# Cross attention, row maximum: from one subtraction on VectorE to the bias of eight exponentials on ScalarE

## The reference

```
ln_out = _ln(hidden_states, ln_w, ln_b)
qx = _ln(_fp8_linear_pertensor(ln_out, wqx, ...).reshape(b, s, g, hpg, d), qxln_w, qxln_b)
kx, vx = jnp.split(jnp.einsum('bsi,oi->bso', cond, w_kv_x), 2, axis=-1)
kx = _ln(kx.reshape(b, sc, g, d), kxln_w, kxln_b)
scores = jnp.einsum('bsghd,btgd->bghst', q, k) * scale      # scale = d ** -0.5, d = 128
p = jax.nn.softmax(scores, axis=-1)                         # over 64 keys
xout = jnp.einsum('bghst,btgd->bsghd', p, v)
catq = _div_clamp_fp8(cat, proj_smooth)                     # then the output projection
```

## Time and profile before

| | us |
|---|---|
| median of 3 runs | 748.12 |
| the profiled execution | 748.93 |
| its span (first to last instruction) | 747.2 |
| PE busy | 613.6 (82%) |
| DVE busy | 505.7 (68%) |
| ACT busy | 378.6 (51%) |
| POOL busy | 359.5 (48%) |
| mean granted PE clock, full = 1 | 0.914 |

### The profile page before, as it was taken

One profiled execution on the slowest core, in us unless ns is written; L12 is line 12 of the kernel. 1 busy time (PEld: TensorE's weight loads), 2 busy tenths in 40 slices (PEclk: granted clock), 3 DMA queues, 4 the chain that ended last, 5 costly groups with the idle time before them and its releaser, 6 DMA issues. The chain is left out here.

```text
span 747.2 us, 10815 instructions
## 1 busy us (share of the span) xinstructions
PE 613.6 (82%) x3735; PEld 492.0 (66%) x3738; DVE 505.7 (68%) x945; ACT 378.6 (51%) x663; POOL 359.5 (48%) x288
## 2 busy tenths in 40 slices
PE   4677996587787999999988788888863599999994
PEld 2544334443566788887877777778763578888883
DVE  5689767694587888888888798888852253333432
ACT  1545666862683655556567366666510333333420
POOL 3321444000656656657468765555631644445541
PEclk9897998698798999999999799999985599999998
DMA  7940211023320010201551111111001211111001
GB/s 258 308 145 14 100 76 49 16 100 128 113 85 1 29 57 1 85 2 52 174 170 25 49 49 51 57 58 57 2 0 53 75 43 43 43 43 42 0 1 57
DMA packets 36212, 50.66 MB, mean 68 GB/s; under 512 B 8257, under 2 KB 22465, under 8 KB 36161
## 3 DMA queue, kind: packets, MB, share of 16 engines
q1 hardware_dynamic: 36160, 50.00, 20.2%
HBM read 37.41 MB, written 12.58 MB: 67 GB/s over the span
## 5 line engine op out<-in xcount | busy, mean ns | idle before, releaser
L1236 POOL TENSOR_TENSOR g_rs<-g_ve,neg_half 128x4 f32<-128x4 f32 x96 | 100.5, 1053 | 98.3 <-DVE g_ve L1309 82.8
L1638 PE MATMUL g_proj<-w_hi,g_xqc 128*128 128x512 f32 x192 | 86.9, 453 | 8.0 <-POOL g_xqc L1231 5.5
L1247 POOL TENSOR_TENSOR g_cat<-g_big,g_kb 128x1024 fp32r<-128x1024 bf16 x32 | 68.4, 2138 | 43.9 <-DVE g_big L1359 43.2
L1309 DVE TENSOR_REDUCE g_ve<-g_sq 128x4 f32<-128x516 f32 x96 | 64.4, 681 | 31.2 <-ACT g_sq L1471 31.2
L1661 PE MATMUL g_turn<-ident,g_qn 128*128 128x128 f32 x384 | 59.6, 282 | 24.9 <-DVE g_qn L1315 12.8
L1638 PE MATMUL g_proj<-w_lo,g_xqc 128*128 128x512 f32 x192 | 79.8, 415 | 0.0
L1672 PE MATMUL g_scores<-g_qkT 128*128 128x64 f32 x512 | 66.6, 287 | 13.0 <-DVE g_ex L1325 13.0
L1672 PEld LDWEIGHTS g_scores<-g_qkT 128*128 128x128 f32 x512 | 64.9, 205 | 18.4 <-issue 18.0
L1900 POOL TENSOR_TENSOR m_h_lo<-m_h,m_h_hi 128x512 fp32r<-128x512 f32 x32 | 40.7, 1289 | 70.7 <-ACT m_h_hi L1947 70.7
L1471 ACT ACTIVATE g_sq<-g_proj 128x512 f32<-128x512 f32 x80 | 47.8, 598 | 49.0 <-PE g_proj L1638 46.0
L1661 PEld LDWEIGHTS g_turn<-ident,g_qn 128*128 128x128 f32 x384 | 44.8, 144 | 37.1 <-DVE g_qn L1315 16.0
(11 more groups left out here) (214 smaller groups left out, 1648.9 us busy)
## 6 DMA issues: line engine op xcount, KB each, us to landing
kvx_rows<-f_kept SPq DMA_DIRECT2D x32, 256.0 KB, 2.4
g_kraw<-kvx_rows SPq DMA_DIRECT2D x16, 256.0 KB, 3.2
g_v<-kvx_rows SPq DMA_DIRECT2D x8, 512.0 KB, 4.6
m_raw<-in_L_W SPq DMA_DIRECT2D x16, 256.0 KB, 3.5
c_raw<-in_L_wqT SPq DMA_DIRECT2D x4, 512.0 KB, 8.8
f_w_ctx<-in_L_wkvxT SPq DMA_DIRECT2D x4, 512.0 KB, 7.7
x_raw<-in_L_wqxT SPq DMA_DIRECT2D x4, 512.0 KB, 3.7
c_praw<-in_L_wprojT SPq DMA_DIRECT2D x4, 512.0 KB, 6.4
```

The lines of the kernel that those rows point to most:

```text
L1236: G.tensor_tensor(rs[:, i % 2, :], ve[:, i % 2, :], k["half"][:, 0:4], ALU.pow).then_inc(q["rs_done"], 1)
L1247: G.tensor_tensor(cat[:, h].rearrange("p h (b s) -> p b h s", b=2), big[:, h, :].rearrange("p (b h s) -> p b h s", b=2, s=SEQ), kb[:, h, : ...
L1309: V.tensor_reduce(ve[:, i % 2, :], sq[:, i % 2], AX.X, ALU.add).then_inc(q["ve_done"], 1)
L1638: last = T.matmul(bank(n, i)[:], xqc[:, n % 2, view * KT + c_, :], w[:, c_, :], start=c_ == 0 and part == 0, stop=c_ == KT - 1 and part == 1)
```

## The change

For cross tiles alone, `less_max` keeps its reduction, but in place of the subtraction it multiplies the 8 maxima by -d^-0.5 in place, which makes them a bias. `exponent` then runs eight exponentials, one for each block of 64 columns, each of which reads the scores from PSUM with its own column of `g_mx` as bias. The last of the eight raises `exp_done`. The bank of scores is now free when ACT has read it, so for cross tiles `scores` waits for `exp_done` where it waited for `sub_done`. The wait for `pt_done` (that the earlier content of `g_ex` has been transposed) goes from DVE to ACT.

```diff
                     V.tensor_reduce(mx[:, h, :], s3, AX.X, ALU.max).then_inc(q["max_done"], 1)
                     dve.wait_ge(q["max_done"], n * 2 + h + 1)
+                    if cross(n):
+                        V.tensor_scalar(mx[:, h, :], mx[:, h, :], -(D ** -0.5), None, ALU.mult).then_inc(q["sub_done"], 1)
+                        return
                     if n > 0:
                         dve.wait_ge(q["pt_done"], n * 2 + h - 1)
...
                 def exponent(n, h):
                     act.wait_ge(q["sub_done"], n * 2 + h + 1)
+                    if cross(n):
+                        act.wait_ge(q["pt_done"], n * 2 + h - 1)
+                        for g in range(2 * GH):
+                            at = slice(g * SEQ, (g + 1) * SEQ)
+                            last = A.activation(ex[:, h, at], sp_[:, at], ACT.Exp, bias=mx[:, h, g:g + 1], scale=D ** -0.5)
+                        last.then_inc(q["exp_done"], 1)
+                        return
                     A.activation(ex[:, h, :], ex[:, h, :], ACT.Exp, scale=D ** -0.5).then_inc(q["exp_done"], 1)
...
                 def scores(n, h):
                     pe.wait_ge(q["tev_done"], n * NN + (h + 1) * NN // 2)
-                    if n > 0 or h > 0:
+                    if cross(n if h > 0 else n - 1):
+                        pe.wait_ge(q["exp_done"], n * 2 + h)
+                    elif n > 0 or h > 0:
                         pe.wait_ge(q["sub_done"], n * 2 + h)
```

## The result

| | before | after |
|---|---|---|
| median of 4 runs each | 747.75 us (746.99 to 748.54) | 784.08 us (782.76 to 787.28) |
| profiled execution | 748.93 | 785.01 |
| its span | 747.2 | 783.3 |
| mean granted PE clock | 0.914 | 0.896 |

The changed kernel is slower by a factor of 1.049 (95% interval 1.046 to 1.053). The forecast was 784 us.

The account below looks back on a forecast made before the run. A cross-tile loop over DVE and PE was taken to bound the kernel, neither engine alone. Wait 20.7, tile 8 2.3, clock 12.5 and 0.6 make 36.1 us on 748.12: 784 us, own range 777 to 791, with rivals 765 to 793.

Parts of the forecast that it names:

- The loop: Cross tile: half 0's reduction and subtraction, PE from second scores to transpose, then DVE; delaying those scores lengthens it one for one.
- the rival on the faster side: Cross tiles: DVE's own work sets the tile and 8.3 us of it are gone, 739.8 us; chance 0.015.
- Step 1: Half 0's multiplication on DVE in cross tiles is held until POOL's running g_cat ends: 1.6 us instead of 0.17.
- near 0.2 for half 1: Sign in the profile after: half 1's multiplication takes near 0.2 us, against about 1.6 us for half 0.
- Step 2: ACT's eight exponentials of 64 columns, starting 0.244 us apart, take 2.04 us where one took 0.63.
- The rival without overlap: ACT's eight exponentials do not overlap: 5.3 us more, 789 us; chance 0.06.
- Step 3: Reduction's start to PE's second scores grows from 1.56 to 4.52 us: 2.96 us per tile, 20.7 over tiles 9 to 15.
- Step 4: Tile 8: DVE's wait ends with POOL, whose root ends later, so the scaling starts 2.3 us later.
- Step 5: PE's clock falls after a 3.4 us gap: 2.5 us in each of tiles 10 to 14, 12.5; tiles 9 and 15, 0.6.
- The sum: Whole kernel: 20.7 + 2.3 + 12.5 + 0.6 = 36.1 us more, added to the median of 748.12.
- the signs: Profile after, cross tiles: tile of 25 to 26 us, clock 0.50 in each tile's scores, DVE's second-scaling wait about 6 us.

Follow-up runs that it names:

- Experiment 4: Kernel before, with PE's scores in cross tiles waiting for the exponential of the half before instead of the subtraction: 753.9 us, ratio 1.009.
- experiment 5: Kernel before, with the change made in half 1 of cross tiles alone; half 0 keeps subtraction, one exponential and early release: 747.6 us, ratio 1.000.
- experiment 1: Changed kernel, with the multiplication of the 8 maxima on ACT instead of DVE: 762.1 us, ratio 1.020 to the kernel before.
- experiment 2: Kernel before, with the multiplication of the maxima added on DVE in cross tiles, its result unread: 766.2 us, ratio 1.027.
- experiment 3: Kernel before, with the 512-column exponential in cross tiles cut into eight of 64 on SBUF without bias, subtraction kept: 747.75 us, ratio 1.000.
- experiment 11: Changed kernel, with 24 unread matmuls filling PE's gap before the second scores in tile 8 too, besides tiles 9 to 14: 768.6 us, ratio 1.028.
- Experiment 6: Changed kernel, with 24 unread matmuls filling PE's gap before the second scores of tiles 9 to 14: 772.3 us, ratio 1.032 to the kernel before.
- 7: Changed kernel, with one exponential of 512 columns in place of the eight, first block's maximum as bias for all: 773.7 us, ratio 1.034.

## Why the prediction was right, step by step

- **The loop.** Right. Experiment 4 moved the release by 0.66 us and the tile by 0.67; experiment 5 left both alone and the time with them. The 0.5 us less work of DVE in each half 1 brought nothing there, and in the changed kernel DVE stands still for 6.8 us of a tile; the rival on the faster side falls with that.
- **Step 1, the hold.** Right in size: 1.60 us on record, to 0.02 us after POOL's end. Shown from both sides: taken away (experiment 1) and added to the kernel before (2). The exclusive lock of the Trainium skill (SBUF — State Buffer, Who interferes with whom) agrees with these rows. The sign "near 0.2 for half 1" held in seven of the eight tiles and not in tile 8 (1.02 us), where the hold was overlooked. What runs here do not show is which condition of the instruction puts it under the lock.
- **Step 2, the exponentials.** The mechanism was right, but the term of 2.04 us was too large: it measured 1.74. One takes 0.33 us as the sum had it, but they start (1.74 - 0.33) / 7 = 0.20 us apart, not 0.244. Without a bias column, from SBUF, they took 1.28 (experiment 3). The estimate from the budget of the Trainium skill (ScalarE: Activation LUTs, Rules for kernel authors), 2.8 us, was further off. The rival without overlap is out.
- **Step 3, the wait.** 4.24 - 1.56 = 2.68 us per tile for 2.96 predicted, by step 2's 0.3. In tiles 9 to 15 that is 18.8 for 20.7. One sign was wrong: DVE's wait before its second scaling was to be about 6 us and is 3.87, since another 2.30 us are spent ahead of the second reduction.
- **Step 4, tile 8.** 4.2 us for 2.3. POOL's delay alone is 27.05 - 25.33 = 1.7 (experiment 11); the other 2.5 are the clock, which I had at 0 there, with 2.3 as its upper end.
- **Step 5, the clock.** Right. It fell in all five of tiles 10 to 14, and the stream grew by 1.55 + 3.11 + 2.70 + 3.10 + 2.65 = 13.1 us for 12.5. One sign was only partly met: the clock was not at 0.50 over the scores of each tile. They took 3.64 us in tiles 12 and 14, but 2.40 to 2.89 in 10, 11 and 13, and tile 10 as a whole took 24.33 us, below the 25 to 26 of the signs. Experiment 6 removed the clock's share without touching the wait.
- **The sum** of 36.1 us met the 36.1 of the spans to the tenth partly by chance: the wait was 1.9 too large, tile 8 with 1.9 too small, the clock 0.6 too small; tiles 9 and 15 took 1.3 beyond the wait where I had 0.6, nearly all of it in tile 15; and 1.3 us came off ahead of tile 8. What lies outside the cross tiles is hardly an effect of the change. Of tile 15's 1.3 us, 0.6 are in its stream and 0.7 come after the attention has ended (DVE's last `g_big`), in code that is the same in all these kernels and took from 183.4 (experiment 2) to 185.2 us (the changed kernel).

## What to carry to other kernels

Before work is moved between engines, find the loop that sets the time and ask of each edit whether it lies on it: the same edit was free in half 1 alone and cost 36 us with half 0. An operation's price is that of the place where it stands; a VectorE instruction on 8 columns took 0.17, 1.02 or 1.60 us by what GpSimd was running, so look in the trace for its form next to the same neighbour. And a longer wait of TensorE may have to be paid twice, once as such and once in the clock afterwards.

## What the hardware showed that I had not expected

- TensorE's clock fell after much shorter gaps than the 3.1 us of the changed kernel, in some tiles and not in others: at 1.74 us in two of five tiles (experiment 1), at 1.94 and 2.07 us in three of five (2, 7), at 1.1 us in none (4). Each count is from one profiled execution.
- Matmuls whose result nobody reads made the kernel faster: 24 per tile in the gap, 12 us (experiment 6).
- Exponentials of 64 columns start 0.15 us apart without a bias column from SBUF, and 0.20 us with one from PSUM (experiments 3 and 5).
